# Graph attention layer on one core: where the score products of two of eight edge slots are summed

## The chip, the cores and the metric

One core of a Trainium2 chip runs the whole layer in one launch. The metric is the device time of the launch in microseconds (us). Differences of under 0.3% are taken as no change.

## What is computed

The layer is attention over the edges of a graph, then a feed-forward block, with normalizations around both. There are L = 4096 rows of C = 512 channels in 8 heads of 64, and E = 131072 edges, sorted by their target row `src`; `dst` names the row that an edge reads.

```python
q = (z @ Wq + bq).reshape(L, H, D); k = ...; v = ...      # z = layernorm(x)
scores = jnp.einsum('ehd,ehd->eh', q[row], k[col]) * scale + bias
m = jax.ops.segment_max(scores, row, num_segments=L)
p = jnp.exp(scores - m[row])
alpha = p / jax.ops.segment_sum(p, row, num_segments=L)[row]
out = jax.ops.segment_sum(alpha[:, :, None] * v[col], row, num_segments=L)
x = x + out.reshape(L, C) @ Wo + bo
x = x + silu(layernorm(x) @ W1 + b1) @ W2 + b2            # then two more residual/norm steps
```

## The kernel before

**First phase** (up to about 1,450 us): edges are sorted into padded records, rows are ranked by their number of edges, and q and a table `kv` (k beside v, 4 KB a row) are written to memory. The change touches it only by a few constants that VectorE makes at the very start.

**Second phase**: 32 tiles of 128 rows, one row a partition. A tile goes through its edges in groups of 8 slots (one edge of each row a slot), so many groups as its widest row needs, at least three; there are 145 groups. Each engine has its own instruction stream, in program order, and they meet at semaphores. For a group:

1. GpSimd gathers 8 slots of `kv` rows into one of three buffers (L523, eight indirect DMAs).
2. VectorE multiplies the keys by q, two slots at a time: four instructions of 128x1024 (L993, `products`). After the second and the fourth it releases TensorE (`PRODS[0]`, `PRODS[1]`).
3. TensorE sums the 64 channels of each head (`sum_d`, L1333). A transpose is a matmul with `ident`; 16 of them accumulate on one bank, each taking every fourth channel, so that the product of 4 slots x 8 heads x 4 partial sums comes out on 128 partitions. `sum_d(0)` does slots 0 to 3, `sum_d(1)` slots 4 to 7. Between the two stands `turn_sum` (L1361, four transposes of the weighted values of the group before).
4. ScalarE copies both results out (L678), and `turn_scores` (L1341) turns them back and adds the 4 partial sums by a matmul with `fold`.
5. VectorE adds the bias, takes the maximum with the running one, and subtracts it (`softmax`: L1039, L1041, L1043); L1039 waits for `turn_scores`. Then the next group's products follow.
6. ScalarE takes the exponentials (L689, L690) and weighs the values of slots 0, 1, 6, 7 (L706, 16 small instructions for each pair). VectorE weighs slots 2 to 5 (L1004), after the next group's products. TensorE sums the weighted slots (`sum_v`, L1351).
7. VectorE rescales the running sum when TensorE has turned it (`scale`, L1012 waits for L1361), and updates the sum of weights (L1017, L1019).

The code of a group is written for four stages: stage 0, 1 and 2 are the first, second and third group of a tile, and stage 3 every later one. Work of earlier tiles is put among them. On TensorE: `down` (L1400) after stage 0, `turn_z2` ahead of stage 1, `up(0)` (L1392) and `turn_att` after stage 1, `up(1)` and `out_proj` (L1376) after stage 2. On VectorE: a copy of q (L1108) ahead of the products of stage 0, then `silu` (L1051) and, behind its softmax, `middle` (a norm) and `residual`; in stage 1 `take_y` and `finish`; in stage 2 `silu`, and behind its softmax `last_norm`. "Issue" in a row of VectorE is mostly the register work of its sequencer between two instructions.

Of the kernel before, what the change touches and what calls it, by code (L numbers as in the profile page):

```python
# [10 lines left out]
ALU = mybir.AluOpType  # L11
ACT = mybir.ActivationFunctionType
AX = mybir.AxisListType

P = 128
HEADS = 8
GROUP = 8
SUB = GROUP // 2
# [18 lines left out]
def layer_kernel(nc, x, src, dst, edge_bias, Wq, bq, Wk, bk, Wv, bv, Wo, bo, ln1_g, ln1_b,  # L37
# [4 lines left out]
    D = C // HEADS  # L42
# [11 lines left out]
    SH = SUB * HEADS  # L54
    FOLD = P // SH
# [19 lines left out]
    with ExitStack() as ctx:  # L75
        def sb(name, shape, dt=F32):
            return ctx.enter_context(nc.sbuf_tensor(name, shape, dt))
# [64 lines left out]
        iota_f = part(P)  # L142
# [17 lines left out]
        prods = part(GROUP * C).rearrange("p (s c) -> p s c", s=GROUP)  # L160
        vw = part(GROUP * C).rearrange("p (s c) -> p s c", s=GROUP)
        scT_sb, vT_sb = part(2 * P), part(C)
# [7 lines left out]
        ones_bf = sb("ones_bf", [3, P], BF16)  # L170
        ident = sb("ident", [P, P])
        fold = sb("fold", [P, SH])
        quarter_f = sb("quarter_f", [P, 1])
        quarter_i = sb("quarter_i", [P, 1], I32)
        eps_t = sb("eps_t", [P, 1])
        offs = sb("offs", [HI, 1])
# [24 lines left out]
        sc = sb("sc", [P, GROUP + 1, HEADS])  # L201
# [7 lines left out]
        bank = [singles[0], wide_ps[1][:, 0, :], singles[1], singles[2], singles[3], wide_ps[0][:, 0, :], wide_ps[0][:, 1, :], wide_ps[1][:, 1, :]]  # L209
# [2 lines left out]
        turn_ps = bank[2]  # L212
        rows_ps = bank[0][:, SIDE * LO:SIDE * LO + NT * 4]
        qkv_ps = [bank[3], bank[4], bank[3]]
        scT_ps, sc_ps = bank[0][:, 0:2 * P], bank[0][:, 2 * P:2 * P + 2 * SH]
        vT_ps, acc_ps = bank[1], bank[7]
        wo_ps, q_ps = turn_ps, bank[3]
        h_ps = bank[5:7]
# [12 lines left out]
        S = {n: sem(n) for n in names}  # L231
# [8 lines left out]
        PRODS = [S["prods_a"], S["prods_b"]]  # L240
# [540 lines left out]
        def _(dve):  # L781
# [19 lines left out]
            dve.tensor_copy(side_f[:, :], side_i[:, :])  # L801
            dve.tensor_scalar(shifted[:, :], iota_f[:, :], -float(HI), part_f[:, 0:1], ALU.add, ALU.is_equal)
            dve.tensor_scalar(fold[:, :], iota_f[:, 0:SH], quarter_f[:, 0:1], None, ALU.is_equal)
            dve.tensor_scalar(ident[:, :], iota_f[:, :], part_f[:, 0:1], None, ALU.is_equal)
            dve.tensor_scalar(tri[:, :], iota_f[:, :], part_f[:, 0:1], None, ALU.is_lt)
            dve.tensor_scalar(triT[:, :], iota_f[:, :], part_f[:, 0:1], None, ALU.is_gt)
# [179 lines left out]
            def products():  # L986

                kv_in = slots(at)
                dve.wait_ge(S["scT_ready"], groups)
                for pair in range(PAIRS):  # L990
                    of = slice(2 * pair, 2 * pair + 2)
                    dve.wait_ge(LANDED[pair], now)
                    last = dve.tensor_tensor(prods[:, of, :], kv_in[:, of, 0:C],  # L993
                                             q_ps[:, :].unsqueeze(1).broadcast_to([P, 2, C]), ALU.mult)
                    if pair % 2:
                        last.then_inc(PRODS[pair // 2], 1)

            def weigh():

# [35 lines left out]

            def softmax(bias):

                dve.wait_ge(S["sc_summed"], groups)
                dve.tensor_tensor(sc[:, 1:GROUP + 1, :], sc_ps.rearrange("p (s h) -> p s h", s=GROUP), bias, ALU.add)  # L1039
                dve.drain()  # L1040
                dve.tensor_reduce(m_run[:, :], sc[:, :, :].rearrange("p s h -> p h s"), AX.X, ALU.max)  # L1041
                dve.drain()
                dve.tensor_tensor(sc[:, :, :], sc[:, :, :], m_run[:, :].unsqueeze(1).broadcast_to([P, GROUP + 1, HEADS]),  # L1043
                                  ALU.subtract).then_inc(S["sc_ready"], 1)
                dve.drain()
# [59 lines left out]
            def body(t, stage):  # L1105
                if stage == 0:
                    hold(S["q_loaded"], t * 16 + 16)
                    dve.tensor_copy(q_ps[:, :], row_q[:, bass.ds(dve.snap(q_at, min_val=0, max_val=C), C)])  # L1108
                    dve.drain()
                products()  # L1110
                if stage == 0:
                    with dve.If(t > 0):
                        weigh()
                        scale()
                        add_weights()
                        dve.drain()
                    with dve.If(t > 2):
                        dve.reg_add(oldest, oldest, 1)
                        silu(dve.snap(oldest), 1)
                    dve.memset(sc[:, 0, :], FLOOR)  # L1120
                else:
                    weigh()
                    dve.tensor_copy(sc[:, 0, :], m_run[:, :])
                if stage == 1:
                    with dve.If(t > 2):
                        take_y(dve.snap(oldest), summed(dve.snap(dve.snap(q_at) * -1 + C)))
                    with dve.If(t > 0):
                        finish(t)
                    first_weights()
                    dve.drain()  # L1130
                if stage == 2:
                    scale()
                    add_weights()
                    with dve.If(t > 1):
                        silu(dve.snap(older), 0)
                    dve.drain()
                if stage == 3:
                    scale()
                    add_weights()
                    dve.drain()  # L1140
                dve.reg_add(groups, groups, 1)
                dve.reg_add(now, now, 1)
                dve.reg_mov(was, at)
                dve.reg_mov(at, dve.snap(dve.snap(dve.snap(at) + HALF) % (RING * HALF)))
                if stage == 2:
                    dve.reg_mov(coming, count_after(dve, t))
                if stage < 3:
                    page_in = rec_all[:, bass.ds(dve.snap(front, min_val=0, max_val=FRONT), FRONT), 0:HEADS]
                    softmax(page_in[:, stage * GROUP:(stage + 1) * GROUP, :])
                else:  # L1150
                    dve.reg_mov(bias_at, off)
                    dve.reg_add(off, off, GROUP)
                    dve.reg_sub(page_left, page_left, 1)
                    with dve.If(dve.snap(page_left) < 1):
                        dve.reg_mov(off, dve.snap(dve.snap(late) + 2 * FRONT))
                        dve.reg_mov(late, dve.snap(dve.snap(late) * -1 + FRONT))
                        dve.reg_mov(page_left, PEEL)
                    softmax(rec_all[:, bass.ds(dve.snap(bias_at, min_val=0, max_val=4 * FRONT - GROUP), GROUP), 0:HEADS])
                if stage == 0:
                    with dve.If(t > 1):  # L1160
                        dve.reg_add(older, older, 1)
                        middle(dve.snap(older))
                        with dve.If(t > 3):
                            dve.reg_add(sent, sent, 16)
                            hold(S["out_sent"], dve.snap(sent))
                        residual(summed(q_at))
                    dve.nop()
                if stage == 2:
                    with dve.If(t > 2):
                        other = dve.snap(dve.snap(q_at) * -1 + C)  # L1170
                        last_norm(bass.ds(dve.snap(nc.s_assert_within(t - 3, 0, NT - 4, skip_runtime_bounds_check_because="the If has t > 2")), 1),
                                  summed(other))
                    dve.nop()
# [41 lines left out]
        def _(pe):  # L1215
            pe.wait_ge(S["keys_ready"], 1)

            for i, of in enumerate((src_f, hi_f)):
                for b in range(TB):
                    last = pe.transpose(bank[2 * i + b // 4][:, (b % 4) * P:(b % 4 + 1) * P], of[:, b * P:(b + 1) * P], ident[:, :])  # L1220
# [22 lines left out]
            for side in range(2):  # L1243
                last = pe.matmul(hist_ps[:, side * SIDE * LO:(side + 1) * SIDE * LO], ident[:, side * HI:(side + 1) * HI], hist_f,
                                 start=True, stop=True)
# [75 lines left out]
            for sem_of in ("y_taken", "y_done", "z2_turned", "acc_ready", "summed0", "summed1", "summed2", "summed3"):  # L1321
                pe.sem_inc(S[sem_of], 1)

            prod_cols = prods.rearrange("p s (h j i) -> p i (s h) j", h=HEADS, j=FOLD)

            def sum_d(a):

                if a == 0:
                    pe.wait_ge(S["scT_sb_ready"], groups)
                    pe.wait_ge(S["sc_ready"], groups)  # L1330
                pe.wait_ge(PRODS[a], now)
                for i in range(D // FOLD):
                    last = pe.matmul(scT_ps[:, a * P:(a + 1) * P], prod_cols[:, i, a * SH:(a + 1) * SH], ident[:, :],  # L1333
                                     start=i == 0, stop=i == D // FOLD - 1, is_transpose=True)
                if a == 1:
                    last.then_inc(S["scT_ready"], 1)

            def turn_scores():
                pe.wait_ge(S["scT_sb_ready"], now)
                for a in range(2):  # L1340
                    last = pe.matmul(sc_ps[:, a * SH:(a + 1) * SH], scT_sb[:, a * P:(a + 1) * P], fold[:, :], start=True, stop=True)  # L1341
                last.then_inc(S["sc_summed"], 1)

            def sum_v(pair):

# [159 lines left out]
```

## Time and profile before

| | |
|---|---|
| median of three runs | 3630.55 us (3626.34 to 3639.14) |
| the profiled execution | 3641.99 us, its span 3640.2 us |
| TensorE matmuls, share of the span | 78%; in the second phase see the rows |
| VectorE | 73% |
| GpSimd | 65% |
| ScalarE | 48% |
| DMA engines: gathers and row loads issued by GpSimd | 47.3% of 16 engines' span |
| chain that ended last, largest shares | TensorE 36%, GpSimd 18%, issue 17%, VectorE 8% |

The shares are means over both phases, which have different limits: the first phase stops at about 1,450 us, and all of the change lies in the second. A stretch of the second phase repeats exactly, tile after tile, so one tile of each size is enough to read.

### The profile page before, as it was taken

The page shows a single profiled execution, that of the slowest core. Times are in us where ns is not written, and L with a number is a line of the kernel's source. Part 1 is how long each engine was busy: PE and PEld are TensorE (multiplying, and loading weights), DVE is VectorE, ACT ScalarE, POOL GpSimd, SP SyncE. Part 2 cuts the span into 40 slices and gives each one's busy share as a digit, 9 for nine tenths or more (in the row PEclk, how much of TensorE's full clock was granted, in tenths as well). Part 3 has the DMA queues.
Part 4 walks back from the last instruction along what each step waited for, and adds up shares of the span by engine and source line. Part 5 has one row for each costly group of instructions (what it writes and reads, how often), then busy time and mean ns, then how long its engine had stood idle before and what let it go on. Part 6 is the DMA issues. An engine that isn't in the chain of part 4 may idle for free.

```text
span 3640.2 us, 82566 instructions
## 1 busy us (share of the span) xinstructions
PE 2834.3 (78%) x18693; PEld 2174.2 (60%) x18694; DVE 2639.6 (73%) x6460; ACT 1731.9 (48%) x6572; POOL 2353.1 (65%) x2550
## 2 busy tenths in 40 slices
PE   8566765666666666377888889888989898988997
PEld 6333333333333333377777777777777777777775
DVE  9677776677676667376777777777777777777774
ACT  0111111111111111276767777777777776777764
POOL 0377777777777777666666666666666666666650
PEclk9967676676766666698999999999999999999999
DMA  7222232322232322877888788788788888788780
GB/s 277 84 81 75 80 90 78 81 74 78 78 91 76 81 74 71 297 274 250 281 301 286 267 283 292 272 279 299 239 287 279 294 281 285 272 292 280 241 278 24
DMA packets 285667, 719.24 MB, mean 198 GB/s; under 512 B 86899, under 2 KB 103475, under 8 KB 285382
## 3 DMA queue, kind: packets, MB, share of 16 engines
q0 software_dynamic: 211776, 585.54, 47.3%
q1 hardware_dynamic: 73862, 133.41, 11.7%
q14 instruction: 22, 0.18, 0.0%
q8 instruction: 7, 0.11, 0.0%
HBM read 717.02 MB, written 72.97 MB: 217 GB/s over the span
## 4 chain that ended last, share of the span: by engine, by line
PE 36%; POOL 18%; issue 17%; DVE 8%; ACT 7%; DMA 7%; DVEq 3%; ACTq 2%; POOLq 1%; PEld 0%; SPq 0%; PEldq 0%
POOL records L410 17%; PE bank L1333 13%; ACT region_c L706 7%; PE wide L1392 6%; PE wide L1400 6%; DMA records<-region_c,pos_i 6%; PE bank L1376 3%; PE wide L1351 3%; DVE region_c L993 2%; PE bank L1232 2%; PE wide L1361 2%; POOL region_a L523 1%; ACTq L706 1%; DVE region_c L941 1%; ACTq L745 1%
## 5 line engine op out<-in xcount | busy, mean ns | idle before, releaser
L523 POOL DMA_INDIRECT region_a<-kv,cols x1160 | 1160.7, 1001 | 513.4 <-issue 456.7
L410 POOL DMA_INDIRECT records<-region_c,pos_i x1024 | 1011.5, 988 | 460.8 <-issue 293.3
L706 ACT ACTIVATE region_c<-region_a,pr 128x64 f32 x4640 | 1155.8, 337 | 44.0 <-issue 44.0
L993 DVE TENSOR_TENSOR region_c<-region_a,bank 128x1024 f32<-128x1024 f32 x580 | 671.1, 1217 | 96.2 <-issue 59.0
L1333 PE MATMUL bank<-ident,region_c 128*128 128x128 f32 x4640 | 620.4, 291 | 135.9 <-DVE region_c L993 131.7
L1333 PEld LDWEIGHTS bank<-ident,region_c 128*128 128x128 f32 x4640 | 591.1, 198 | 161.7 <-issue 151.0
L1351 PE MATMUL wide<-ident,region_c 128*128 128x128 f32 x4640 | 568.9, 276 | 77.5 <-ACT region_c L706 77.5
L1351 PEld LDWEIGHTS wide<-ident,region_c 128*128 128x128 f32 x4640 | 516.7, 144 | 111.2 <-ACT region_c L706 111.0
L628 ACT COPY region_c<-region_a 128x64 f32 x128 | 32.5, 254 | 1032.2 <-DMA records<-region_c,pos_i 1032.2
L1290 PE MATMUL bank<-region_b,region_a 128*128 128x512 f32 x768 | 496.2, 806 | 0.0
L1277 PE MATMUL wide<-region_c 64*128 64x64 f32 x2048 | 193.3, 345 | 202.1 <-issue 184.2
L1277 PEld LDWEIGHTS wide<-region_c 64*128 64x128 f32 x2048 | 174.4, 251 | 289.7 <-issue 289.7
L1290 PEld LDWEIGHTS bank<-region_b,region_a 128*128 128x128 f32 x768 | 191.4, 262 | 256.4 <-issue 256.4
L1004 DVE TENSOR_TENSOR region_c<-region_a,bank 128x1024 f32<-128x1024 f32 x290 | 340.3, 1215 | 1.1 <-issue 1.1
L906 DVE SCALAR_TENSOR_TENSOR region_c<-region_a,region_c 128x128 bf16<-128x128 int16 x1024 | 292.4, 350 | 24.0 <-issue 24.0
L678 ACT COPY region_c<-bank 128x256 f32<-128x256 f32 x145 | 54.0, 372 | 475.6 <-PE bank L1333 475.6
L1392 PE MATMUL wide<-region_c,region_b 128*128 128x128 f32 x2048 | 239.2, 275 | 3.2 <-ACT region_c L716 3.2
L1392 PEld LDWEIGHTS wide<-region_c,region_b 128*128 128x128 f32 x2048 | 233.6, 192 | 3.7 <-ACT region_c L716 3.7
L1400 PE MATMUL wide<-region_b,region_c 128*128 128x512 f32 x512 | 225.0, 592 | 0.0
L924 DVE TENSOR_TENSOR pos_i<-region_c 128x8 int32<-128x8 f32 x128 | 21.4, 168 | 272.1 <-DMA records<-region_c,pos_i 267.3
L1297 PE MATMUL bank<-ident,region_a 128*128 128x128 f32 x128 | 35.7, 434 | 190.9 <-DVE region_a L938 190.9
L1232 PE MATMUL bank<-region_c 128*64 128x64 bf16 x2048 | 180.1, 318 | 0.6 <-DVE region_c L826 0.6
(186 smaller groups left out, 3278.2 us busy)
## 6 DMA issues: line engine op xcount, KB each, us to landing
region_a<-srcT SPq DMA_DIRECT2D x128, 256.0 KB
region_a<-kv,cols POOLq DMA_INDIRECT x1160, 5.8
region_a<-hiT SPq DMA_DIRECT2D x256, 64.0 KB
x_rows<-region_c SPq DMA_DIRECT2D x32, 512.0 KB, 3.4
records<-region_c,pos_i POOLq DMA_INDIRECT x1024
kv<-region_a SPq DMA_DIRECT2D x32, 512.0 KB
records<-region_c SPq DMA_DIRECT2D x32, 480.0 KB, 14.7
region_a<-in_x_dram SPq DMA_DIRECT2D x32, 256.0 KB, 3.2
```

Of the source, the lines that this page charges most:

```text
L410: pool.indirect_dma_start(records, bass.IndirectOffsetOnAxis(ap=pos_i[j % 2][:, s:s + 1], axis=0), rec_w[j % 2][:, s, :], None).then_inc(S ...
L523: pool.indirect_dma_start(KV[r][:, s, :], None, kv, bass.IndirectOffsetOnAxis(ap=cols[r][:, s:s + 1], axis=0), bounds_check=L - 1, oob_is_ ...
L706: last = act.activation(vw[:, s, of], v_part[:, s, C + hd * D:C + (hd + 1) * D], ACT.Copy, scale=pr[:, s + 1, hd:hd + 1])
L906: last = dve.scalar_tensor_tensor(eq[:, s * P:(s + 1) * P], srcb[b][:, s * P:(s + 1) * P], src_f[:, bass.ds(st * STREAMS + s, 1)], tri[:, ...
L993: last = dve.tensor_tensor(prods[:, of, :], kv_in[:, of, 0:C], q_ps[:, :].unsqueeze(1).broadcast_to([P, 2, C]), ALU.mult)
L1004: dve.tensor_tensor(vw[:, s:s + 2, :].rearrange("p s (h d) -> p s h d", h=HEADS), kv_in[:, s:s + 2, C:2 * C].rearrange("p s (h d) -> p s h ...
L1277: last = pe.matmul(wide_ps[b][:, side, s * LO:(s + 1) * LO], hitT[b][rows, s * P:(s + 1) * P], table_sb[rows, s * LO:(s + 1) * LO], start= ...
L1290: last = pe.matmul(qkv_ps[w][:, :], zT1[:, c * P:(c + 1) * P], Wqkv[:, w, c, :], start=False, stop=c == KT - 1)
L1333: last = pe.matmul(scT_ps[:, a * P:(a + 1) * P], prod_cols[:, i, a * SH:(a + 1) * SH], ident[:, :], start=i == 0, stop=i == D // FOLD - 1, ...
L1351: last = pe.matmul(vT_ps[:, c * P:(c + 1) * P], vw[:, s, c * P:(c + 1) * P], ident[:, :], start=s == 0 and c == 0, stop=s == GROUP - 1, is ...
L1392: last = pe.matmul(h_ps[m // 4][:, (m % 4) * P:(m % 4 + 1) * P], W1_sb[:, c, m * P:(m + 1) * P], z2T[:, c * P:(c + 1) * P], start=c == 0, ...
L1400: last = pe.matmul(y_ps[:, :], hT[:, m * P:(m + 1) * P], W2_sb[:, m, :], start=m == 0, stop=m == HT - 1)
```

## The change

VectorE sums slots 6 and 7 itself: a reduction of 128x1024 products to 16 scores a row, and an addition of their bias, both put ahead of the wait for `sc_summed` in `softmax`. `sum_d(1)` now has slots 4 and 5 alone, with 8 partial sums for each score: 8 transposes, not 16, that take every eighth channel. It needs only the third product instruction, so `PRODS[1]` is released there. A second constant matrix `fold_far` (128x16) adds 8 partial sums, and `turn_scores` yields 48 columns, not 64. In stage 0 one drain of VectorE is added behind the memset of the running maximum. At the start four small instructions make the constants.

```diff
@@ setup on VectorE
+            dve.tensor_scalar(quarter_i[:, :], quarter_i[:, :], 1, None, ALU.arith_shift_right)
+            dve.drain()
+            dve.tensor_copy(eighth_f[:, :], quarter_i[:, :])
+            dve.drain()
+            dve.tensor_scalar(fold_far[:, :], iota_f[:, 0:SH // 2], eighth_f[:, 0:1], None, ALU.is_equal)
@@ products()
-                    if pair % 2:
-                        last.then_inc(PRODS[pair // 2], 1)
+                    if pair in (1, 2):
+                        last.then_inc(PRODS[pair - 1], 1)
@@ softmax(bias)
+                far = sc[:, GROUP - 1:, :]
+                dve.tensor_reduce(far, prods[:, GROUP - 2:, :].rearrange("p s (h d) -> p s h d", h=HEADS), AX.X, ALU.add)
+                dve.drain()
+                dve.tensor_tensor(far, far, bias[:, GROUP - 2:, :], ALU.add)
                 dve.wait_ge(S["sc_summed"], groups)
-                dve.tensor_tensor(sc[:, 1:GROUP + 1, :], sc_ps.rearrange("p (s h) -> p s h", s=GROUP), bias, ALU.add)
+                dve.tensor_tensor(sc[:, 1:GROUP - 1, :], sc_ps.rearrange("p (s h) -> p s h", s=GROUP - 2), bias[:, 0:GROUP - 2, :], ALU.add)
@@ body(), stage 0, VectorE
                     dve.memset(sc[:, 0, :], FLOOR)
+                    dve.drain()
@@ TensorE
+            prod_far = prods[:, SUB:SUB + 2, :].rearrange("p s (h j i) -> p i (s h) j", h=HEADS, j=2 * FOLD)
@@ sum_d(a)
-                for i in range(D // FOLD):
-                    last = pe.matmul(scT_ps[:, a * P:(a + 1) * P], prod_cols[:, i, a * SH:(a + 1) * SH], ident[:, :],
-                                     start=i == 0, stop=i == D // FOLD - 1, is_transpose=True)
+                parts = D // FOLD // (a + 1)
+                for i in range(parts):
+                    of = prod_far[:, i] if a else prod_cols[:, i]
+                    last = pe.matmul(scT_ps[:, a * P:(a + 1) * P], of, ident[:, :],
+                                     start=i == 0, stop=i == parts - 1, is_transpose=True)
@@ turn_scores()
-                for a in range(2):
-                    last = pe.matmul(sc_ps[:, a * SH:(a + 1) * SH], scT_sb[:, a * P:(a + 1) * P], fold[:, :], start=True, stop=True)
-                last.then_inc(S["sc_summed"], 1)
+                pe.matmul(sc_ps[:, 0:SH], scT_sb[:, 0:P], fold[:, :], start=True, stop=True)
+                pe.matmul(sc_ps[:, SH:SH + SH // 2], scT_sb[:, P:2 * P], fold_far[:, :], start=True, stop=True).then_inc(S["sc_summed"], 1)
```

On VectorE, in the code of a stage 3 group, from the second value product to the end of `softmax`, the kernel before has these rows (`sc` holds the scores, `region_c` here products, bias and weights, `bank` PSUM; ISA is a register instruction).

```order
L1004 TENSOR_TENSOR region_c<-region_a,bank 128x1024
L1123 COPY sc<-m_run 128x8
L1012 TENSOR_TENSOR wide<-wide,pr 128x512
L1017 TENSOR_TENSOR pr<-l_run,pr 128x8
L1019 TENSOR_REDUCE l_run<-pr 128x8
L1141 ISA
L1151 ISA
L1154 COMPARE_AND_BRANCH
L1155 ISA
L1154 UNCONDITIONAL_BRANCH
L1039 ISA
L1039 TENSOR_TENSOR sc<-bank,region_c 128x64
```

The changed kernel has these from the update of the sum of weights on; the lines are numbered 12 higher here.

```order
L1026 TENSOR_REDUCE l_run<-pr 128x8
L1153 ISA
L1163 ISA
L1166 COMPARE_AND_BRANCH
L1167 ISA
L1166 UNCONDITIONAL_BRANCH
L1046 TENSOR_REDUCE sc<-region_c 128x16
L1048 ISA
L1048 TENSOR_TENSOR sc<-sc,region_c 128x16
L1050 ISA
L1050 TENSOR_TENSOR sc<-bank,region_c 128x48
```

The reduction, a register instruction and the small addition stand between the register work and the addition that waits for TensorE.

On TensorE, in the code of a stage 2 group, the scores' way is this in the kernel before.

```order
L1333 MATMUL bank<-ident,region_c 128x128 x16
L1361 MATMUL wide<-ident,region_c 128x128 x4
L1333 MATMUL bank<-ident,region_c 128x128 x16
L1341 MATMUL bank<-fold,region_c 128x32 x2
L1351 MATMUL wide<-ident,region_c 128x128 x16
```

In the changed kernel it is this.

```order
L1348 MATMUL bank<-ident,region_c 128x128 x16
L1375 MATMUL wide<-ident,region_c 128x128 x4
L1348 MATMUL bank<-ident,region_c 128x128 x8
L1355 MATMUL bank<-fold,region_c 128x32
L1356 MATMUL bank<-fold_far,region_c 128x16
L1365 MATMUL wide<-ident,region_c 128x128 x16
```

Eight transposes of the second `sum_d` are gone, and the order of the rest is as it was.

## Rows read from the trace of the kernel before

**Rows 1.** busy time by window: engines in the page's order, clock, DMA share, GB/s
```profile
1500.00:3600.00 2100.00, 1853.08 (x13405) 1601.21 (x13406) 1580.43 (x2850) 1492.39 (x5864) 1322.36 (x1497) 0.97 0.79 274
```

**Rows 2.** waits of VectorE, 1500 to 3600: total us, times, longest
```profile
DVE sc L1039 <- PE bank L1341: 153.5, 115, 4.7
DVE wide L1012 <- PE wide L1361: 60.8, 41, 4.8
DVE region_c L993 <- SPq L368: 28.2, 24, 3.8
```

**Rows 3.** timeline, VectorE, a four-group tile: start, duration, instruction, idle before
```profile
2845.72 0.21 DVE L1039 TENSOR_TENSOR sc<-bank,region_c 128x64 f32<-128x64 f32 x1
2862.56 0.23 DVE L1039 TENSOR_TENSOR sc<-bank,region_c 128x64 f32<-128x64 f32 x1 [0.58 <-issue]
2872.09 0.70 DVE L1012 TENSOR_TENSOR wide<-wide,pr 128x512 f32<-128x512 f32 x1 [1.34 <-PE wide L1361]
2891.54 0.22 DVE L1039 TENSOR_TENSOR sc<-bank,region_c 128x64 f32<-128x64 f32 x1 [1.90 <-PE bank L1341]
2903.80 0.21 DVE L1039 TENSOR_TENSOR sc<-bank,region_c 128x64 f32<-128x64 f32 x1
```

**Rows 4.** timeline, TensorE, the same tile
```profile
2848.91 7.03 PE L1400 MATMUL wide<-region_b,region_c 128*128 128x512 f32 x16
2860.88 0.63 PE L1341 MATMUL bank<-fold,region_c 128*128 128x32 f32 x4 [0.46 <-ACT region_c L678]
2902.23 0.63 PE L1341 MATMUL bank<-fold,region_c 128*128 128x32 f32 x4 [0.46 <-ACT region_c L678]
```

**Rows 5.** timeline, VectorE, a tile of five groups and the group before it
```profile
2525.32 0.22 DVE L1039 TENSOR_TENSOR sc<-bank,region_c 128x64 f32<-128x64 f32 x1 [1.18 <-PE bank L1341]
2539.58 0.23 DVE L1039 TENSOR_TENSOR sc<-bank,region_c 128x64 f32<-128x64 f32 x1 [1.66 <-PE bank L1341]
2566.71 0.70 DVE L1012 TENSOR_TENSOR wide<-wide,pr 128x512 f32<-128x512 f32 x1 [1.89 <-PE wide L1361]
2611.17 0.23 DVE L1039 TENSOR_TENSOR sc<-bank,region_c 128x64 f32<-128x64 f32 x1 [1.71 <-PE bank L1341]
```

**Rows 6.** timeline, TensorE, the same stretch
```profile
2523.87 0.63 PE L1341 MATMUL bank<-fold,region_c 128*128 128x32 f32 x4 [0.46 <-ACT region_c L678]
2531.28 3.65 PE L1333 MATMUL bank<-ident,region_c 128*128 128x128 f32 x16 [2.49 <-DVE region_c L993]
2535.58 2.74 PE L1333 MATMUL bank<-ident,region_c 128*128 128x128 f32 x16
```

**Rows 7.** timeline, VectorE, first later group of an early tile
```profile
1633.07 0.23 DVE L1039 TENSOR_TENSOR sc<-bank,region_c 128x64 f32<-128x64 f32 x1 [0.98 <-issue]
```

**Rows 8.** windows with L1039 alone (one run of it is one group)
```profile
1500.00:1750.00 250.00, 4.27 (x19) 0.91 0.77 281
1750.00:2662.00 912.00, 14.39 (x64) 0.96 0.81 282
2662.00:3482.00 820.00, 12.46 (x56) 0.99 0.81 279
```

**Rows 9.** windows with L1108 alone (one run of it is one tile)
```profile
1750.00:2662.00 912.00, 9.03 (x13) 0.96 0.81 282
2662.00:3482.00 820.00, 9.72 (x14) 0.99 0.81 279
```

**Rows 10.** instructions by line, 1500 to 3600: busy us, mean ns, idle before us
```profile
L1004 DVE TENSOR_TENSOR region_c<-region_a,bank 128x1024 f32<-128x1024 f32 x290 | 340.3, 1215 | 1.1 <-issue 1.1
L1017 DVE TENSOR_TENSOR pr<-l_run,pr 128x8 f32<-128x8 f32 x113 | 18.9, 167 | 0.0
L1333 PE MATMUL bank<-ident,region_c 128*128 128x128 f32 x4640 | 620.4, 291 | 135.9 <-DVE region_c L993 131.7 <-issue 4.2
```

**Rows 11.** instructions by line, 0 to 1500, VectorE
```profile
L921 DVE TENSOR_REDUCE region_c<-region_c 128x8 f32<-128x512 f32 x128 | 88.0, 688 | 11.7
L839 DVE TENSOR_REDUCE region_c<-region_c 64x64 f32<-64x512 f32 x1 | 1.0, 1003 | 0.1
```

More of the change, by code:

```diff
@@ L172, in layer_kernel @@
         fold = sb("fold", [P, SH])
+        fold_far = sb("fold_far", [P, SH // 2])
         quarter_f = sb("quarter_f", [P, 1])
+        eighth_f = sb("eighth_f", [P, 1])
         quarter_i = sb("quarter_i", [P, 1], I32)
@@ L214, in layer_kernel @@
         qkv_ps = [bank[3], bank[4], bank[3]]
-        scT_ps, sc_ps = bank[0][:, 0:2 * P], bank[0][:, 2 * P:2 * P + 2 * SH]
+        scT_ps, sc_ps = bank[0][:, 0:2 * P], bank[0][:, 2 * P:2 * P + 3 * SH // 2]
         vT_ps, acc_ps = bank[1], bank[7]
@@ L1322, in _ @@
                 pe.sem_inc(S[sem_of], 1)
-            prod_cols = prods.rearrange("p s (h j i) -> p i (s h) j", h=HEADS, j=FOLD)
+            prod_cols = prods[:, 0:SUB, :].rearrange("p s (h j i) -> p i (s h) j", h=HEADS, j=FOLD)
+            prod_far = prods[:, SUB:SUB + 2, :].rearrange("p s (h j i) -> p i (s h) j", h=HEADS, j=2 * FOLD)
             def sum_d(a):
```

## The prediction

> **What bounds the kernel now.** First the busy shares of the gathering part, where the whole change lies [rows 1]: of 2100 us TensorE's matmuls fill 1853, VectorE 1580, ScalarE 1492, GpSimd 1322, and the DMA engines are at 0.79. By that view TensorE is the bound, and taking 8 of its 32 score transposes a group looks like a gain. Shares don't tell which wait ends last, so next came VectorE's waits [rows 2]: in 145 groups it waited 153.5 us at L1039 for the scores, 60.8 us at L1012 for the turned sum, and 28.2 us for gathers. These 242 us look like room for work on VectorE. Whether they are is decided in the timeline, by what stands ahead of each wait.
>
> A tile of four groups lasts 58.08 us, from the L1039 at 2845.72 to that at 2903.80 [rows 3]. At 2902.23 TensorE starts the last scores, they end at 2902.86, and L1039 starts 0.94 us later [rows 4]. Where TensorE really comes last (in stage 3 of this tile, and in stage 0 of the next kind) the step takes 0.17 us. So here VectorE was 0.77 us late: it is itself the bound, although the view of waits may name TensorE. The same in stage 1: scores end at 2861.51 and L1039 starts at 2862.56, 0.88 us late; its idle of 0.58 us is register work [rows 3, 4]. In this tile VectorE truly waits in two places only: 1.34 us at L1012 in stage 2, and in stage 3 a part of the 1.90 us at L1039. What part is seen in an early tile, where TensorE had long been done: there 0.98 us of register work remained ahead of the same L1039 [rows 7]. So 0.92 us is wait. True room: 1.34 + 0.92 = 2.26 us in a tile of four groups, 0.57 us a group.
>
> A tile of five groups lasts 71.59 us (2539.58 to 2611.17) [rows 5]. In its fifth group L1039 starts 0.82 us after the scores' end at 2524.50 [rows 5, 6]: the idle of 1.18 us that the view puts down to TensorE is nearly all register work. Room: at stage 0 all of the 1.71 us (in the four-group tile that L1039 has no idle ahead of it at all [rows 3]), 1.89 us at L1012 in stage 2, 0.92 us at L1039 in stage 3 as above, and about 0.3 us in two small waits at L1012 (an estimate, from what is left between neighbouring starts). Together 4.8 us, 0.96 a group.
>
> So two engines alternate as the bound, and in more than half of the groups VectorE is it.
>
> **What is removed.** Eight of 32 transposes a group. In the five-group tile 16 of them at half rate took 2.74 and 3.65 us [rows 6]; at full rate the mean record is 291 ns, but they overlap, and 4640 of them fill 620 us, which is 0.134 us each [rows 10]. Eight save TensorE 0.9 to 1.1 us a group. `sum_d(1)` may also start one product earlier, and L1039 is 16 columns shorter (0.02 us). All that lets the scores come earlier. It is worth something only where VectorE waits for them.
>
> **What is added on VectorE, each group.**
> - The reduction of 128x1024 to 16. The nearest rows: a reduction of 512 took 688 ns [rows 11], and an instruction of the same 1024 columns took 1215 ns [rows 10]. I take 1.22 us. Lower bound 1.15; upper 1.38, twice the reduction of 512. The reduction with 64 results took 1003 ns for 512 [rows 11], 315 ns more for 56 more results, so 8 more results may cost 0.05.
> - Between the reduction and the small addition a drain and a register instruction: 0.2 us. No row has just this pair; bounds 0.08 and 0.3, estimates from the spacing of L1039, L1041 and L1043 and from the 0.33 to 0.6 us that longer register work takes.
> - The addition of 16 columns: 0.17 us, as L1017 with 8 [rows 10]. The next instruction starts about 0.1 us before such a one ends, so 0.07 on the path, less 0.02 for the shorter L1039.
>
> Sum: 1.22 + 0.20 + 0.07 - 0.02 = 1.47, call it 1.45 us a group, bounds 1.3 and 1.7. The drain in stage 0 gives 0.08 a tile, and the constants at the start 0.5 us once, part of it beside the first loads.
>
> [...]
>
> **The sum.** The work stands ahead of L1039 in VectorE's stream. Where VectorE was late it is added in full; where it waited it fills the wait first. Everything behind it on VectorE, the next products above all, moves with it, and TensorE waits for these.
> - Four-group tile: 4 x 1.45 + 0.08 - 2.26 = +3.6 us. There are 15: 56 groups in 14 tiles, and one among the 13 tiles before them [rows 8, 9].
> - Five-group tile: 5 x 1.45 + 0.08 - 4.8 = +2.5 us. There are 12 (64 groups in 13 tiles, one of them of four).
> - The last two tiles, of three groups: 3 x 1.45 + 0.08 - 1.6 (their L1012 wait) = +2.8 each.
> - The first three tiles, 19 groups [rows 8], are paced by gathers: 26.5 of the 28.2 us of waits for gathers fall there, and 19 x 1.45 = 27.6 us fits into these, if each wait meets the work in its own group. I take +5, between 0 and 28.
>
> 15 x 3.6 + 12 x 2.5 + 5.6 + 5 + 0.5 = +95 us, or 0.65 us a group. The profiled execution took 3641.99 us, which is 11.4 above the median of the three runs; on that execution the sum would give 3737, and on the median 3725 us. By the bounds of the price (1.3: 74, 1.7: 131) and of the first tiles (-5, +23) the added time lies between 69 and 154 us, and mostly within 70 to 130.
>
> **Does the wait for TensorE come back?** Where VectorE is slower, TensorE gets idle, and its clock falls: after 2.49 us of idle 16 transposes took 3.65 us, and the second 16 took 2.74 [rows 6], where elsewhere they fill 2.0. In the new kernel this happens after each group in which VectorE runs behind: in stage 0 of nearly all tiles, and in the fifth group. The chain at the lower level in stage 0 was 2531.28 to about 2539.4 (end of the scores); with half of the 2.74 gone it ends 1.2 us earlier, while VectorE arrives at L1039 about 0.2 us before 2539.58 once the 1.45 is added to it. So about 1 us is left, and the fallen clock is hidden, thinly.
>
> **The rivals.**
> 1. VectorE's own work sets the pace, as above: 0.80. Price 70 to 150 us, 3700 to 3780.
> [...]
> 3. The room is real (0.05, faster): the 242 us of waits [rows 2] hold all of 145 x 1.45 = 210 us, and TensorE, the busiest engine, gives its 0.9 us back in each group: -130 us, 3500 us. Against it: 0.77 and 0.88 us of lateness in two of four groups, which no wait can absorb. It decides below a price of about 0.6 us a group, half of the multiplication's time for as many columns.
> 4. A cheap reduction (0.07, within 0.3% or slightly slower): if the reduction ran two columns in the time of one, 0.61 us, the price would be 0.85, and the tiles would give +1.2 and -0.5 us: about +15 us, 3645 us. The 688 ns for 512 speak against it.
>
> Slower by over 0.3%: cases 1, 2 and part of 4, 0.90. Within 0.3% (about 11 us, what a measurement here tells from no change): 0.05. Faster: 0.05. The range reaches from 3690, below the low end of case 1, to 3775.
>
> **What the new profile would show.** The reduction (L1046) 145 times at 1.15 to 1.4 us. A four-group tile of about 61.7 us and a five-group one of 74.1. The first addition behind it (L1050) with almost no idle put down to TensorE. The wait at L1012 in stage 2 gone: before, it was 1.34 us with VectorE 0.88 late and 1.89 where it was less late, so 3.2 us of lateness leave nothing. TensorE's transposes x3480, its waits for the products about doubled, and a lower granted clock. [...]

## The result and the profile after

The changed kernel takes 3737.84 us (median of 4 runs, 3736.48 to 3738.11), the kernel before 3634.62 (4 runs). The ratio is 1.0283, 95% interval 1.0263 to 1.0303: slower by 103 us. The two profiled executions, 3641.99 and 3738.11 us, are 96.1 us apart; 95 were forecast for that pair.

The page of the changed kernel, its parts 1 and 4: busy time of the engines, and shares of the chain that ended last.

```profile
PE 2755.7 (74%) x17533; PEld 2091.2 (56%) x17534; DVE 2827.1 (76%) x6753; ACT 1724.7 (46%) x6572; POOL 2354.9 (63%) x2550
...
DVE 35%; issue 21%; POOL 18%; DVEq 10%; PE 7%; DMA 6%; POOLq 1%; ACT 1%; ACTq 0%; PEld 0%; SPq 0%; PEldq 0%
```

TensorE's share of the chain fell from 36% to 7%, VectorE's rose from 8% to 35%, and that of VectorE's sequencer (DVEq) from 3% to 10%. The stretch from 1500 to 3600 us, to be laid beside [rows 1]:

```profile
1500.00:3600.00 2100.00, 1700.13 (x11672) 1451.09 (x11673) 1701.15 (x3002) 1424.21 (x5627) 1297.74 (x1467) 0.93 0.78 268
```

TensorE and VectorE are now equally busy, and the granted clock fell from 0.97 to 0.93. The waits of the changed kernel, 1500 to 3700 us (total us, times, longest; `issue` is time in which the engine waited for nothing that the profile shows), answer to [rows 2]:

```profile
DVE sc L1046 <- issue: 112.5, 145, 1.2
DVE sc L1048 <- issue: 27.1, 145, 0.2
DVE region_c L1000 <- SPq L370: 12.2, 11, 2.0
DVE wide L1019 <- PE wide L1375: 6.5, 15, 2.4
...
PE bank L1348 <- DVE region_c L1000: 260.4, 86, 42.1
ACT bank L691 <- DVE sc L1054: 138.5, 105, 3.5
```

No wait of VectorE for the scores is among them (L1050, the addition that needs them, has no idle ahead of it in the rows below); before there were 153.5 us. Its wait for the turned sum (L1019, before L1012) fell from 60.8 to 6.5 us, and that for gathers from 28.2 to 12.2. TensorE waits 260 us for products, and ScalarE has a new wait of 138 us for the scores (L691). What stands ahead of the reduction is 112.5 us of VectorE's own register work. The groups of instructions by line (busy us, mean ns, idle before) answer to [rows 10, 11]:

```profile
L1046 DVE TENSOR_REDUCE sc<-region_c 128x16 f32<-128x1024 f32 x145 | 176.9, 1220 | 112.5 <-issue 112.5
L1048 DVE TENSOR_TENSOR sc<-sc,region_c 128x16 f32<-128x16 f32 x145 | 25.9, 178 | 27.1 <-issue 27.1
L1050 DVE TENSOR_TENSOR sc<-bank,region_c 128x48 f32<-128x48 f32 x145 | 30.1, 208 | 0.0
L1348 PE MATMUL bank<-ident,region_c 128*128 128x128 f32 x3480 | 531.5, 312 | 265.8 <-DVE region_c L1000 260.4 <-issue 4.8
```

The reduction took 1220 ns (1.22 us was taken), the register step ahead of the small addition 27.1 / 145 = 0.19 us, the addition 0.18 (178 ns). Now the timeline of the last group of a four-group tile and the first of the next, which ends in stage 0:

```profile
2946.64 1.22 DVE L1046 TENSOR_REDUCE sc<-region_c 128x16 f32<-128x1024 f32 x1 [0.87 <-issue]
...
2948.20 0.21 DVE L1050 TENSOR_TENSOR sc<-bank,region_c 128x48 f32<-128x48 f32 x1
...
2954.15 3.65 PE L1348 MATMUL bank<-ident,region_c 128*128 128x128 f32 x16 [4.95 <-DVE region_c L1000]
...
2957.59 1.06 PE L1375 MATMUL wide<-ident,region_c 128*128 128x128 f32 x4
...
2958.69 0.70 DVE L1019 TENSOR_TENSOR wide<-wide,pr 128x512 f32<-128x512 f32 x1 [0.17 <-PE wide L1375]
...
2960.09 0.69 DVE L1062 SCALAR_TENSOR_TENSOR region_c<-wide,region_c 128x512 f32<-128x512 f32 x1 [0.28 <-issue]
...
2960.73 0.07 DVE L1131 MEMSET sc<- 128x8 f32 x1
...
2961.03 0.38 PE L1356 MATMUL bank<-fold_far,region_c 128*128 128x16 f32 x2
...
2961.25 1.22 DVE L1046 TENSOR_REDUCE sc<-region_c 128x16 f32<-128x1024 f32 x1 [0.46 <-issue]
...
2962.66 0.17 DVE L1048 TENSOR_TENSOR sc<-sc,region_c 128x16 f32<-128x16 f32 x1 [0.19 <-issue]
2962.81 0.21 DVE L1050 TENSOR_TENSOR sc<-bank,region_c 128x48 f32<-128x48 f32 x1
```

TensorE idles 4.95 us ahead of stage 0 and then does 16 transposes in 3.65 us, at a granted clock of 0.50 in 2954.15 to 2957.80; yet its scores end at 2961.41 and VectorE reads them at 2962.81, 1.40 us later. Between the memset and the reduction stand 0.46 us of register work. In the kernel before, L1039 had no idle ahead of it at this place [rows 3]. From the start of the reduction to that of L1050 it is 1.56 us in both groups shown.

**Links.** Since tiles repeat, the links from one group to the next say most: from the start of the subtraction that ends one softmax (L1043, after the change L1054) to the next one's. The table has the smallest link of the 15 four-group tiles ("3 to 3": of the 12 five-group tiles), in us; with "both runs" the smaller of the two. In the groups of runs of e1 to e4, of their repetition and of e8 every kernel took 22 to 24% longer (the kernel before 4459, 4518 and 4513 us), so times of those groups are compared only inside the group.

| kernel | 2 to 3 | 3 to 3 | 3 to 0 | 0 to 1 | 1 to 2 |
|---|---|---|---|---|---|
| before | 16.33 | 10.67 | 12.24 | 16.84 | 12.57 |
| changed | 16.66 | 12.07 | 14.34 | 18.37 | 12.53 |
| e1, drain moved (both runs) | 16.67 | 12.07 | 13.84 | 18.38 | 12.53 |
| e2, TensorE's relief alone (both runs) | 15.25 | 10.67 | 12.24 | 16.85 | 11.14 |
| e3, 16 transposes again (both runs) | 16.66 | 12.07 | 14.34 | 18.38 | 12.53 |
| e4, half a reduction (both runs) | 16.12 | 11.54 | 13.81 | 17.90 | 12.01 |
| e5, before without last drain | 16.42 | 10.35 | 12.24 | 16.84 | 12.49 |
| e6, reduction over registers | 15.86 | 11.10 | 13.84 | 18.01 | 11.43 |
| e7, e6 without last drain | 15.75 | 10.94 | 13.84 | 18.01 | 11.24 |
| e8, stage 2 alone | 14.99 | 10.35 | 12.24 | 16.84 | 11.82 |

### The profile page after: what moved, and what is told of

It is laid out like the page before. It is cut to its first block, busy times and chain, and to the rows that moved or that the text cites. A ratio compares the mean times of both kernels' runs of the same rounds, so it can differ in the third digit from the quotient of the medians.

```text
span 3736.3 us, 80863 instructions
## 1 busy us (share of the span) xinstructions
PE 2755.7 (74%) x17533; PEld 2091.2 (56%) x17534; DVE 2827.1 (76%) x6753; ACT 1724.7 (46%) x6572; POOL 2354.9 (63%) x2550
## 4 chain that ended last, share of the span: by engine, by line
DVE 35%; issue 21%; POOL 18%; DVEq 10%; PE 7%; DMA 6%; POOLq 1%; ACT 1%; ACTq 0%; PEld 0%; SPq 0%; PEldq 0%
POOL records L412 17%; DVE region_c L1000 10%; DMA records<-region_c,pos_i 5%; DVE region_c L1011 5%; DVE sc L1046 4%; PE bank L1244 2%; DVEq L1025 2%; PE bank L1348 2%; DVE wide L1019 1%; POOL region_a L525 1%; DVEq L1071 1%; DVE region_c L1062 1%; DVE root_t L1091 1%; DVE m_run L1052 1%; DVE region_c L948 1%
## 5 line engine op out<-in xcount | busy, mean ns | idle before, releaser
L1348 PE MATMUL bank<-ident,region_c 128*128 128x128 f32 x3480 | 531.5, 312 | 265.8 <-DVE region_c L1000 260.4
L1348 PEld LDWEIGHTS bank<-ident,region_c 128*128 128x128 f32 x3480 | 492.5, 201 | 306.4 <-issue 306.0
L1365 PE MATMUL wide<-ident,region_c 128*128 128x128 f32 x4640 | 576.9, 279 | 74.4 <-ACT region_c L708 74.4
L1365 PEld LDWEIGHTS wide<-ident,region_c 128*128 128x128 f32 x4640 | 526.1, 146 | 106.7 <-ACT region_c L708 106.7
L1302 PE MATMUL bank<-region_b,region_a 128*128 128x512 f32 x768 | 487.4, 793 | 0.0
L1046 DVE TENSOR_REDUCE sc<-region_c 128x16 f32<-128x1024 f32 x145 | 176.9, 1220 | 112.5 <-issue 112.5
```

The costliest lines, as they stand in the source:

```text
L1046: dve.tensor_reduce(far, prods[:, GROUP - 2:, :].rearrange("p s (h d) -> p s h d", h=HEADS), AX.X, ALU.add)
L1302: last = pe.matmul(qkv_ps[w][:, :], zT1[:, c * P:(c + 1) * P], Wqkv[:, w, c, :], start=False, stop=c == KT - 1)
L1348: last = pe.matmul(scT_ps[:, a * P:(a + 1) * P], of, ident[:, :], start=i == 0, stop=i == parts - 1, is_transpose=True)
L1365: last = pe.matmul(vT_ps[:, c * P:(c + 1) * P], vw[:, s, c * P:(c + 1) * P], ident[:, :], start=s == 0 and c == 0, stop=s == GROUP - 1, is ...
```

## The experiments

The kernels were run in four groups, each beside the kernel before; the changed kernel itself ran in none of them. In the traces of e1 to e4 and e8 engines stand still now and then (see the end), so most links are longer than they need be, but some tiles hold links that nothing holds up. These experiments are read by their smallest links. Between the two groups, and with the undisturbed kernels where VectorE paces, these agree to 0.03 us, with two exceptions: the link 2 to 3 of e4 (16.24 and 16.12; its five-group tiles give 16.13 in both), and the link 1 to 2 of e2, told there. The expectations of the second run of e1 to e4 put the longer times down to gathers, and that was wrong.

**e1: what the added drain costs.**

```diff
                     with dve.If(t > 0):
                         weigh()
                         scale()
                         add_weights()
                         dve.drain()
+                    dve.drain()
                     with dve.If(t > 2):
                         dve.reg_add(oldest, oldest, 1)
                         silu(dve.snap(oldest), 1)
                     dve.memset(sc[:, 0, :], FLOOR)
-                    dve.drain()
```

> The changed kernel with the drain of stage 0 moved from behind the memset to ahead of silu, where VectorE has just drained anyway. Theory A (that drain keeps about 0.4 us of register work from running beside silu, and stage 0 is paced by VectorE): a tile is 0.4 us shorter in stage 0, 12 to 15 us in all, about 3724 us. Theory B (a drain costs its own 0.08 us, as I predicted): 2 to 3 us, about 3735 us.

> The same kernel as in the first call, where all kernels ran with slow gathers (the kernel before at 4459 us); there stage 0 was 13.85 us after stage 3 in undisturbed tiles, 0.5 less than in the changed kernel. Theory A: 14 to 20 us less than the changed kernel, about 3721 us. Theory B: 2 to 3 us less.

Against the kernel before in the same group: 0.9878 (0.9818 to 0.9937) and 0.9913 (0.9878 to 0.9948), at 4396 and 4478 us. These can't be set beside the changed kernel's 1.0283. The link from stage 3 to 0 fell from 14.34 to 13.84 us, and no other moved. The timeline of e1 in stage 0:

```profile
3493.62 0.69 DVE L1062 SCALAR_TENSOR_TENSOR region_c<-wide,region_c 128x512 f32<-128x512 f32 x1 [0.33 <-issue]
3494.24 1.21 DVE L1046 TENSOR_REDUCE sc<-region_c 128x16 f32<-128x1024 f32 x1
```

The reduction now follows `silu` with no idle: the register work runs beside `silu`. The drain cost 0.50 us a tile, 16 us in 31 tiles (an estimate from the link), and not 0.08 us a tile. Theory A, by the link; the 3724 us were not measured. e6, which moves this drain too and ran undisturbed, has the same 13.84 us.

**e2: TensorE's relief alone.** The kernel before; `sum_d(1)` does half of its transposes and leaves half of the channels of slots 4 to 7 out.

```diff
-                for i in range(D // FOLD):
+                parts = D // FOLD // (a + 1)
+                for i in range(parts):
```

> The kernel before with sum_d(1) doing 8 of its 16 transposes and VectorE untouched (half of the channels of slots 4 to 7 is left out of the scores). It shows what TensorE's relief alone is worth. Theory A (VectorE is the bound in more than half of the groups, its true waits are 2.3 us in a four-group tile and 4.8 in a five-group one): gain limited to these waits, a part kept by the fallen clock of stage 0: 60 to 90 us, about 3560 us. Rival (TensorE is the bound in each group): 0.9 us a group, 130 us, about 3500 us.

> The same kernel again, at the usual speed of gathers. Theory A: gain limited to VectorE's true waits, 60 to 90 us, about 3560 us. Rival (TensorE is the bound in each group): 130 us, about 3500 us.

Ratios 0.9852 (0.9806 to 0.9898) and 0.9907 (0.9877 to 0.9936), inside their groups. The links 3 to 3, 3 to 0 and 0 to 1 stand as before to 0.01 us: TensorE's 0.9 us are worth nothing there. 2 to 3 is 1.08 us shorter, in several tiles of both runs. 1 to 2 is 11.14 us, against 12.57, in a single tile of the first run; the next smallest is 14.68 there, and 12.75 in the second run. So the relief is shown to pay in one of the four links of a four-group tile, and it may pay in a second. In five-group tiles the link 3 to 0, which held the 1.71 us of wait before, has no undisturbed case in these traces. The gain of 60 to 90 us at the usual speed stays unmeasured.

**e3: the changed kernel with 16 transposes again.** TensorE does its second sum twice, the second time anew.

```diff
-                for i in range(parts):
+                for again in range(a + 1):
+                    for i in range(parts):
...
```

> The changed kernel, but TensorE does the 8 transposes of its second sum twice over (the second round starts the sum anew), so that it has 16 again, as before the change, while VectorE still reduces its two slots. Theory A (after the change VectorE alone paces): TensorE's relief is worth nothing there, 0 to 10 us slower than the changed kernel, 3738 to 3748 us. Rival (the relief is paid out, and the loss is its difference to VectorE's price): 100 to 130 us slower, about 3850 us.

> The same kernel again, at the usual speed of gathers. Theory A: 0 to 10 us above the changed kernel, 3738 to 3748 us. Rival: 100 to 130 us above it.

Ratios 1.0070 (1.0027 to 1.0113) and 1.0042 (1.0014 to 1.0070), inside their groups. By lines, e3 has the transposes of the kernel before and the reductions of the changed one:

```profile
L1349 PE MATMUL bank<-ident,region_c 128*128 128x128 f32 x4640 | 650.8, 298 | 198.8 <-issue 133.0 <-DVE region_c L1000 65.4
L1046 DVE TENSOR_REDUCE sc<-region_c 128x16 f32<-128x1024 f32 x145 | 176.9, 1220 | 112.6 <-issue 112.6
```

All five links are those of the changed kernel to 0.01 us. In a tile that nothing holds up, what the change took from TensorE is worth nothing once the reduction is on VectorE. Over a whole run of these groups it was worth something: in the first, e3 stands 87 us above e1 (75 without its three longest runs), in the second 62, and the moved drain explains about 16 of it. The forecast of 0 to 10 us holds for the links; as a time beside the changed kernel it was not measured.

**e4: half of the reduction.** The reduction leaves half of the channels of its two slots out.

```diff
-... prods[:, GROUP - 2:, :].rearrange("p s (h d) -> p s h d", h=HEADS), AX.X, ALU.add)
+... prods[:, GROUP - 2:, :].rearrange("p s (h d) -> p s h d", h=HEADS)[:, :, :, 0:D // 2], AX.X, ALU.add)
```

> The changed kernel with VectorE's reduction over half of the channels of its two slots (512 columns, not 1024; the other half is left out of these scores). Theory A (VectorE is the bound in every group): 0.53 us a group less, 77 us, about 3661 us. Rival (other engines take over as soon as VectorE has some slack): under 40 us.

> The same kernel again, at the usual speed of gathers. Theory A: 0.53 us a group, 77 us less than the changed kernel, about 3661 us. Rival: under 40 us.

```profile
L1046 DVE TENSOR_REDUCE sc<-region_c 128x16 f32<-128x512 f32 x145 | 99.5, 686 | 112.6 <-issue 112.6
```

The reduction went from 1220 to 686 ns, 0.53 us. The links fell by 0.54, 0.53, 0.53, 0.47 and 0.52 us. Where nothing else holds a group up, VectorE paces it, one to one, in all five links. Ratios 0.9898 (0.9867 to 0.9929) and 0.9910 (0.9874 to 0.9945), inside their groups; the 77 us at the usual speed were not measured as a time.

**e5: the kernel before without its last drain.** This and the next two ran in one group, beside the kernel before at 3633.8 us (19 runs).

```diff
                     with dve.If(t > 1):
                         silu(dve.snap(older), 0)
-                    dve.drain()
                 if stage == 3:
                     scale()
                     add_weights()
-                    dve.drain()
```

> The kernel before without the drain that ends the weights' update in stages 2 and 3, so that VectorE's register work can run beside L1012 to L1019. Theory A (in the kernel before VectorE is late only in the fifth and later groups and in stages 0 and 1): it gains 0.6 us in each later stage 3 group and little elsewhere, 10 to 20 us, about 3620 us. Rival (register work is off the path): no change.

3620.39 us (median of 5 runs, one of which took 4665.94), ratio 0.9957 (0.9941 to 0.9973). The time is what theory A forecast; the place is so in part. The link 3 to 3 is 0.32 us shorter, half of what I expected of it; most of the gain lies in the link to stage 0 of the five-group tiles (median 12.89 us, before 14.23). Why that one gives so much is not shown.

**e6: the reduction ahead of the register work.** The changed kernel, with the drain as in e1.

```diff
+                dve.tensor_reduce(sc[:, GROUP - 1:, :], prods[:, GROUP - 2:, :].rearrange(...), AX.X, ALU.add)
                 dve.reg_add(groups, groups, 1)
                 dve.reg_add(now, now, 1)
                 dve.reg_mov(was, at)
...
             def softmax(bias):
                 far = sc[:, GROUP - 1:, :]
-                dve.tensor_reduce(far, prods[:, GROUP - 2:, :].rearrange(...), AX.X, ALU.add)
                 dve.drain()
```

> The changed kernel, the drain of stage 0 moved as in e1, and the reduction issued ahead of the group's register work instead of behind it, so that this work runs beside the reduction. The idle time ahead of the reduction is 112 us in the changed kernel. Theory A (VectorE paces every group, and its register work is on the path): most of this goes, 90 to 115 us less than the changed kernel, 3625 to 3650 us. Rival (only instructions count, register work is hidden elsewhere): no more than the 12 to 15 us of the drain.

3644.8 us, ratio 1.0031 (1.0021 to 1.0041): 93 us of the 103 are back, with the same instructions on the same data. (The changed kernel ran in another group, but the kernel before stood within 1 us in both, 3634.62 and 3633.8.) Two things were moved. About 16 of the 93 are the drain's, by e1; some 77 belong to the place of the reduction (an estimate, by difference).

```profile
L1152 DVE TENSOR_REDUCE sc<-region_c 128x16 f32<-128x1024 f32 x145 | 176.5, 1217 | 9.6 <-issue 0.7
```

The idle time ahead of the reduction fell from 112.5 to 9.6 us. Its duration is the same. Against e1 the links fell by 0.81 (2 to 3), 0.97 (3 to 3), 0.37 (0 to 1) and 1.10 us (1 to 2); the link 3 to 0 stayed, since there e1 had already freed the register work.

**e7: e6 without the last drain**, as in e5.

> As the run with the reduction ahead of the register work, and without the drain that ends the weights' update in stages 2 and 3. Theory A: the reduction starts 0.07 us sooner in 113 groups, 5 to 10 us less than that run. Rival: no change.

3632.33 us, ratio 0.9994 (0.9985 to 1.0004): 12.5 us below e6, where 5 to 10 were expected, and level with the kernel before. The fair neighbour is e5, the kernel before without the same drain, at 3620.39 us: in its best place tried, the change still costs 12 us.

**e8: the change in stage 2 alone.** e5 as the base; the reduction is issued ahead of `scale`, which waits there for the turned sum (1.34 us in the kernel before [rows 3]).

```diff
                 if stage == 2:
+                    far = sc[:, GROUP - 1:, :]
+                    dve.drain()
+                    dve.tensor_reduce(far, prods[:, GROUP - 2:, :].rearrange(...), AX.X, ALU.add)
                     scale()
                     add_weights()
+                    dve.tensor_tensor(far, far, page_at[:, 3 * GROUP - 2:3 * GROUP, :], ALU.add)
...
-                    sum_d(1)
-                    turn_scores()
+                    sum_d(1, stage == 2)
+                    turn_scores(stage == 2)
```

> The kernel before without the last drain (as e5), and with the change's split of the score sums in stage 2 alone, the reduction issued ahead of the instruction that waits there for the turned sum (1.34 us of true wait in a four-group tile, 1.9 in a five-group one). Theory A (work on VectorE is free only inside a true wait, and TensorE's relief pays only where TensorE ends last, that is from stage 2 to stage 3): the link from stage 2 to 3 falls from 16.4 to about 15.4 us, the others stay, 25 to 35 us less than e5 in all, 3585 to 3600 us, ratio to the kernel before about 0.988. Rival (the place makes no difference, each reduction costs its 1.4 us): 31 us more than e5 less the relief, about 3630 us.

4488 us against 4513, ratio 0.9949 (0.9920 to 0.9978), where 0.988 was forecast.

```profile
L1141 DVE TENSOR_REDUCE sc<-region_c 128x16 f32<-128x1024 f32 x32 | 39.0, 1220 | 2.3
```

By the smallest links, the reduction costs nothing where it stands in a wait: 1 to 2 is 11.82 us, where e5 has 12.49, and 2 to 3 is 14.99 against 16.42, while the links of the other stages are e5's. That speaks against the rival. But few tiles show it (the link 2 to 3 is 14.99 us in one four-group tile and 14.93 in two of five groups, and far longer in most others), and a smallest link can hold a lead from a stall before it. So that the change pays in this form is not shown, and the forecast of 3585 to 3600 us is open.

## Why the prediction was right, and where its terms were off

**The bound.** That VectorE already paced many of the groups, although TensorE was the busiest engine and the view of waits named TensorE, carried the forecast. e2 shows it: three of five links don't move when TensorE gets 8 transposes fewer. e3 and e4 show that after the change VectorE paces all five. The words "in more than half of the groups" don't follow from the prediction's own list of waits, which leaves VectorE as the bound in two of four and in two of five groups, 54 of the 120 in these tiles. The sum didn't use them.

**The price.** Forecast 1.45 us a group. The link 3 to 3 grew by 1.40 us and 0 to 1 by 1.53. The pieces were not all right. From the start of the reduction to that of L1050 it is 1.56 us: 1.22 for the reduction, 0.19 for the register step and 0.15 for the addition, of which 0.07 was taken. In turn the register work ahead became shorter, which the sum didn't have: the fifth group had 1.18 us ahead of L1039 [rows 5] and has 1.04 ahead of the reduction.

```profile
2636.12 1.22 DVE L1046 TENSOR_REDUCE sc<-region_c 128x16 f32<-128x1024 f32 x1 [1.04 <-issue]
2637.53 0.17 DVE L1048 TENSOR_TENSOR sc<-sc,region_c 128x16 f32<-128x16 f32 x1 [0.19 <-issue]
2637.68 0.21 DVE L1050 TENSOR_TENSOR sc<-bank,region_c 128x48 f32<-128x48 f32 x1
```

1.56 less 0.14, less 0.02 for the narrower addition, is the 1.40 of the link. That two errors of about 0.1 us cancelled was luck. At 1220 ns the fourth case, a cheap reduction, did not come.

**The true room.** 2.26 us forecast in a four-group tile. The link 2 to 3 grew by 0.33 us only, and 1 to 2 not at all (0.04 shorter): there the waits took the reduction in. With the price of 1.40 us they took 1.07 and 1.44 us, 2.5 together, where 0.92 and 1.34 had been read off the waits.

**The mis-sized term: the drain in stage 0.** The step "the drain in stage 0 gives 0.08 a tile" looked at its own duration (in the kernel before 0.07 us lie between the end of L1039, at 2862.79, and the start of L1041, with a drain between). What it did here is hold back the register work behind it until `silu` and the memset are done: 0.46 us idle in the timeline, 0.50 us by e1, 16 us in all. Over the run it was made up for by differences the other way. From the starts of the subtraction of each tile's first group, the mean four-group tile went from 58.58 to 62.12 us (+3.5, forecast 3.6), the mean five-group tile from 71.09 to 74.21 (+3.1, forecast 2.5), and the first three tiles together lost 4.7 us (forecast 5). The last two tiles lost 2.0 us (forecast 5.6), and what stands ahead of the first of these starts was 1.1 us shorter (forecast 0.5 longer). That adds up to the 96.1. The four-group tiles meet the forecast in part by luck: tiles do not repeat exactly in the kernel before, where 7 of the 15 are 0.8 to 1.5 us longer than the 58.08 of the others, and in the changed kernel that spread is gone (61.93 to 62.26). Against 58.08 the mean grew by 4.0 us, which is the forecast with the drain at 0.50.

**The fallen clock.** Both traces show the low clock behind idle time. In the kernel before, in the stretch of [rows 6], the granted clock is 0.50 while the first 16 transposes run (2531.28 to 2534.93), 0.70 while the second 16 do (2535.58 to 2538.32), which the prediction calls half rate too, and 1.00 from 2539.25 to 2542.07, in the sum of the values. The first score sums of a group, from 1760 us on, by the idle of TensorE ahead of them:

| kernel | idle ahead, us | sums | 16 transposes took, us |
|---|---|---|---|
| before | 1.82 | 15 | 2.04 or 2.05 in ten, 2.45 to 3.51 in five |
| before | 2.48 to 2.56 | 12 | 2.85 to 3.65 |
| changed | 0.30 to 1.71 | 30 | 2.04 or 2.05 |
| changed | 2.79 to 4.04 | 25 | 2.04 and 2.05 in two, 2.54 to 3.65 in 23 |
| changed | 4.93 to 5.11 | 15 | 3.42 to 3.65 |

Sums with no idle ahead took 1.96 to 2.05 us, but for 12 in the kernel before (2.40 to 2.80 us), each right behind a slow first sum. The same idle doesn't always go with the same time, and no run tells why. In the changed kernel TensorE idled 4.95 us ahead of the stage 0 shown and ran its sums at a granted clock of 0.50 (2954.15 to 2957.80) and 0.55 (2958.45 to 2960.33), as forecast; 0.17 us of wait at L1019 was the whole price in this tile, and the scores were there 1.40 us ahead of L1050, 1.23 more than the 0.17 of a release (about 1 was forecast). The granted clock of the stretch from 1500 to 3600 us fell by 0.04. The second case (0.08), a `down` at the low clock, did not come: behind this stage 0 it fills 7.03 us at a granted clock of 1.00 (2965.54 to 2972.57), as in the tile of [rows 6] (2543.54 to 2550.57), and its matmuls have the same mean as before (592 ns).

**The medians.** Between the medians the change costs 103 us, between the two profiled executions 96.1. The agreement of the second with the forecast of 95 is partly luck: the profiled execution of the kernel before was above all of its 19 later runs (median 3633.8, highest 3638.74), that of the changed kernel was an ordinary one. Of the 12 us between the forecast median of 3725 and 3737.84, 4 lie in the median before, which a fourth run moved from 3630.55 to 3634.62, and 8 are forecast too low; the drain alone would account for 13.

**What was not seen.** The forecast took VectorE's register work as given. e6 shows that most of the price, some 77 of the 103 us, hung on where the reduction was issued: behind that work it adds its full length, ahead of it it hides about 0.5 us a group of idle that was there already. The kernel before has such idle ahead of L1039 too, 0.98 to 1.18 us in the later groups [rows 5, 7], and e5 takes a part of it.

## What to carry to other kernels

A wait that the profile puts down to an engine may be the waiter's own register work: compare the end of the releasing instruction with the start of the waiting one, and only the shortest such step (here 0.17 us) is a release. Before work is moved to a less busy engine, sum its true waits over one period of the loop; here they were 0.6 us a group in a four-group tile, and a step of 1.4 did not fit. Where an instruction must be added to a bound engine, try it ahead of the register work, with no drain between them: here that took back most of the loss (e6). A drain can cost what could have run beside it, here 0.50 us (e1), against the 0.08 that was taken for it.

## What the runs showed of the hardware

A reduction of 128x1024 to 16 took 1220 ns, one of 128x512 to 16 took 686, and the row of before for 512 to 8 was 688 [rows 11]: between 512 and 1024 columns the time grows by 1.04 ns for each column read, and 8 or 16 results make no difference. The row of 64 results took 1003 ns for 512 [rows 11]; no run here tells why.

In the traces of e1 to e4 and e8 engines stand still at places where they wait for nothing that the profile shows. In the timeline of e1, first run, matmuls of one sequence of 32 stand apart:

```profile
2411.83 0.27 PE L1406 MATMUL wide<-region_c,region_b 128*128 128x128 f32 x1 [0.71 <-issue]
...
2413.97 0.27 PE L1406 MATMUL wide<-region_c,region_b 128*128 128x128 f32 x1 [1.87 <-issue]
...
2415.42 4.15 PE L1406 MATMUL wide<-region_c,region_b 128*128 128x128 f32 x21 [1.17 <-issue]
...
2415.74 2.35 DVE L1011 TENSOR_TENSOR region_c<-region_a,bank 128x1024 f32<-128x1024 f32 x2 [1.33 <-remote]
2415.78 0.59 ACT L686 COPY region_c<-wide 128x512 f32<-128x512 f32 x1 [3.55 <-remote]
```

In the trace of the kernel before, the same 32 matmuls follow each other without a gap, and the program has them wait only once, ahead of the first.

```profile
2865.63 3.74 PE L1392 MATMUL wide<-region_c,region_b 128*128 128x128 f32 x32
```

Here TensorE has gaps of 0.71, 1.87 and 1.17 us between them, and VectorE and ScalarE stand still in the same stretch, for 1.33 and 3.55 us, for a cause that the profile doesn't name. These gaps are no waits for gathers, since those matmuls need none; and the first phase is longer too: the subtraction of the first softmax starts at 1913 us in e1, at 1511 in the changed kernel. No run shows the cause, and it stays open. What it means for a comparison was seen: e1, which by its links would be about 2.4% slower than the kernel before, was 1.2% and 0.9% faster beside it. The sign of a difference of this size can depend on such stalls.
